# Cross-attention with fake quantisation on one core: TensorE's work grouped by array shape, one accumulator bank, three score banks

## What is computed

```python
q = _fq_sym(q, axis=-1); k = _fq_sym(k, axis=-1); v = _fq_sym(v, axis=2)
attn = jnp.einsum('bhqd,bhkd->bhqk', q, k)
attn = jax.nn.softmax(attn.astype(jnp.float32), axis=-1)
attn = _fq_unsigned(attn, axis=-1)        # round(attn / (rowmax / 255)), clipped to 0..255
out = jnp.einsum('bhqk,bhkd->bhqd', attn, v)
```

## Time and profile before

| | |
|---|---|
| median of 3 runs | 9790.67 us (9786.69 to 9797.47) |
| profiled execution | 9785.63 us, span 9783.8 us |
| TensorE busy by the profile | 9016.5 us, 92% |
| VectorE busy | 6668.5 us, 68% |
| ScalarE busy | 6056.4 us, 62% |
| GpSimd busy | 5207.5 us, 53% |
| DMA | 303.96 MB, mean 31 GB/s |

### The profile page before, as it was taken

How to read it: one execution, slowest core, us unless ns; L and a number is a source line. 1 busy time by engine, 2 the same in 40 slices (tenths; PEclk the granted TensorE clock), 3 DMA queues, 4 the chain that set the end, 5 groups by cost and what they waited for, 6 DMA issues and landing times.

```text
span 9783.8 us, 225157 instructions
## 1 busy us (share of the span) xinstructions
PE 9016.5 (92%) x60844; PEld 2698.2 (28%) x60844; DVE 6668.5 (68%) x6162; ACT 6056.4 (62%) x12203; POOL 5207.5 (53%) x3575
## 2 busy tenths in 40 slices
PE   8935999999999999999999999999999999998688
PEld 4501222222222222222222222222222222222243
DVE  8968777767776777677767776777767776730266
ACT  2300767767676767676767676776767676767333
POOL 5723555555555555555555555555555555555266
PEclk9955999999999999999999999999999999999799
DMA  5662010110101010101010101010110101010100
GB/s 167 198 137 67 10 24 18 22 18 16 25 15 26 10 31 10 31 10 31 10 30 11 30 11 25 16 23 18 19 22 17 25 10 30 11 28 6 26 4 3
DMA packets 305415, 303.96 MB, mean 31 GB/s; under 512 B 50718, under 2 KB 297802, under 8 KB 300458
## 3 DMA queue, kind: packets, MB, share of 16 engines
q1 hardware_dynamic: 304682, 303.13, 14.2%
q10 hardware_dynamic: 672, 0.16, 0.0%
HBM read 226.31 MB, written 76.71 MB: 31 GB/s over the span
## 4 chain that ended last, share of the span: by engine, by line
PE 84%; issue 6%; DVE 5%; ACT 2%; POOL 2%; DMA 1%; SPq 0%; DVEq 0%; ACTq 0%; POOLq 0%
PE psum L1385 32%; PE psum L1354 23%; PE psum L1308 15%; PE psum L1364 8%; DVE mpart L1171 3%; PE psum L1273 2%; ACT y L1068 1%; POOL mix L410 1%; PE psum L670 1%; PE psum L1406 1%; DVE act_c L550 1%; PE psum L1342 1%; PE psum L1344 0%; PE psum L643 0%; PE psum L1285 0%
## 5 line engine op out<-in xcount | busy, mean ns | idle before, releaser
L1171 DVE TENSOR_REDUCE mpart<-psum 128x978 f32 x4992 | 5768.0, 1175 | 2194.0 <-PE psum L1308 2193.3
L1068 ACT ACTIVATE y<-psum 128x400 f32<-128x400 f32 x11520 | 5638.0, 503 | 2338.9 <-PE psum L1385 1875.5
L986 POOL TENSOR_SCALAR xh<-y 128x1600 f16<-128x1600 f32 x2880 | 4397.8, 1527 | 3666.0 <-ACT y L1068 3666.0
L1385 PE MATMUL psum<-QT,K 99*128 x11520 | 3811.3, 344 | 142.3 <-ACT y L1068 62.6
L1354 PE MATMUL psum<-y,ones 128*1 128x400 f32 x23056 | 2517.3, 503 | 0.6 <-ACT y L1068 0.6
L1308 PE MATMUL psum<-K,QS 48*128 48x489 bf16 x9984 | 1974.8, 392 | 266.1 <-DVE mpart L1171 194.8
L1385 PEld LDWEIGHTS psum<-QT,K 99*128 x11520 | 1041.3, 96 | 3722.2 <-issue 3629.4
L1364 PE MATMUL psum<-xh,vwin 128*16 128x400 f16 x11532 | 1000.7, 338 | 0.0
L1308 PEld LDWEIGHTS psum<-K,QS 48*128 48x128 bf16 x9984 | 482.3, 93 | 1366.4 <-issue 791.5
L1354 PEld LDWEIGHTS psum<-y,ones 128*1 128x1 f32 x23056 | 322.0, 81 | 577.8 <-issue 571.4
L1364 PEld LDWEIGHTS psum<-xh,vwin 128*16 128x16 f16 x11532 | 274.7, 85 | 557.2 <-issue 546.1
(11 more groups left out here) (184 smaller groups left out, 2380.1 us busy)
## 6 DMA issues: line engine op xcount, KB each, us to landing
K<-kT_parts SPq DMA_DIRECT2D x204, 240.0 KB, 8.3
vwin<-v_int SPq DMA_DIRECT2D x579, 80.0 KB, 1.9
K<-kT_parts SPq DMA_DIRECT2D x772, 45.8 KB
kT_parts<-part SPq DMA_DIRECT2D x135, 256.0 KB, 3.2
K<-kT_parts SPq DMA_DIRECT2D x102, 242.0 KB, 8.5
src<-in_ctx_dram SPq DMA_DIRECT2D x46, 512.0 KB, 4.5
v_float<-kv SPq DMA_DIRECT2D x45, 512.0 KB, 5.2
vin<-v_float SPq DMA_DIRECT2D x9, 2560.0 KB, 13.1
```

Of the source, the lines that this page charges most:

```text
L986: pool.tensor_scalar(xh[:, g % YR, :, :], y[:, g % YR, :, :], INT_STEP, 0.0, ALU.mult, ALU.add)\
L1068: act.activation(y[:, s % YR, j, :], s2_bank(j), ACT.Exp).then_inc(exp_done, 1)
L1171: dve.tensor_reduce(mpart[:, t, ds(2 * cp + j, 1)], s1_buf(n)[:, :, 0:CHALF], AX.XY, ALU.max)\
L1385: pe.matmul(s2_bank(j), K3[0:MROW, h % 2, ds(c * REGION + t * P, P)], queries, start=True, stop=True).then_inc(s2_ready, 1)
```

## The change

- TensorE's order in a group becomes: two scores, the group's one or two jobs, two scores, sums, values.
- The ring of score banks grows from two to three (`S2_RING`, banks 4 to 6), so that a score waits for the exponential of three tiles before.
- ScalarE takes the exponentials of three tiles with two instructions: one over two banks (800 elements per partition), one over a single bank.
- Sums and values share one accumulator bank (`ACC`, bank 7). The ones become a matrix of 17 columns, 16 of them zero, so that the sum comes out on row 16 of each strip, beside the values' rows 0 to 15, and adds zero to these.
- One copy (`acc_s`) in place of two at a block's start, and one product in place of two for each sequence in `turn_out`.
- Rings of three groups in place of five, lags of 1 and 2 groups in place of 2 and 3.
- The constants at the start are set accordingly.

```diff
-YR = 5
-LAG_SUM, LAG_PV = 2, 3
+YR = 3
+LAG_SUM, LAG_PV = 1, 2
+S2_RING = 3
...
+        def s2_banks(t, count):
+            return psum[:, 4 + t % S2_RING:4 + t % S2_RING + count, 0:QB]
+
         def s2_bank(j):
-            return psum[:, 4 + j % 2, 0:QB]
-
-        PV, SUM = psum[:, 6, 0:QB], psum[:, 7, 0:QB]
+            return psum[:, 4 + j % S2_RING, 0:QB]
+
+        ACC = psum[:, 7, 0:QB]
...
-                for s in range(GROUPS):
-                    if not later and s == LAG_SUM:
+                def group_start(s):
+                    if not later and s == LAG_PV:
 
                         act.wait_ge(summed, YR + groups_before(h, b, 0))
+                        act.wait_ge(pv_done, YR + groups_before(h, b, 0))
                         act.wait_ge(rsum_done, block_of(h, b))
-                        act.activation(sum_s[:], SUM, ACT.Copy).then_inc(evicted, 1)
-                    if not later and s == LAG_PV:
-                        act.wait_ge(pv_done, YR + groups_before(h, b, 0))
-                        act.activation(pv_s[:], PV, ACT.Copy).then_inc(evicted, 1)
+                        act.activation(acc_s[:], ACC, ACT.Copy).then_inc(evicted, 1)
 
                     act.wait_ge(summed, groups_before(h, b, c) + s + 1)
                     act.wait_ge(rounded_y, groups_before(h, b, c) + s + 1)
-                    for j in range(GT):
-                        act.wait_ge(s2_ready, tiles_before(h, b, c) + GT * s + j + 1)
-                        act.activation(y[:, s % YR, j, :], s2_bank(j), ACT.Exp).then_inc(exp_done, 1)
+
+                rows = y[:].rearrange("p r t q -> p (r t) q")
+                for t in range(0, BTILES, S2_RING):
+                    for first, count in ((t, 2), (t + 2, 1)):
+                        for u in range(first, first + count):
+                            if u % GT == 0:
+                                group_start(u // GT)
+                        act.wait_ge(s2_ready, tiles_before(h, b, c) + first + count)
+                        at = first % (YR * GT)
+                        act.activation(rows[:, at:at + count, :], s2_banks(first, count), ACT.Exp).then_inc(exp_done, count)
...
-                    pe.matmul(s1_buf(n)[0:SEQ, 0, 32 * s:32 * s + HD], pv_s[:, s * SEQ:(s + 1) * SEQ], sel[:, 0:HD],
-                              start=True, stop=True, skip_group_check=True)
-                    last = pe.matmul(s1_buf(n)[0:SEQ, 0, 32 * s + HD:32 * s + HD + 1], sum_s[:, s * SEQ:(s + 1) * SEQ],
-                                     sel[:, HD:HD + 1], start=True, stop=True, skip_group_check=True)
+                    last = pe.matmul(s1_buf(n)[0:SEQ, 0, 32 * s:32 * s + HD + 1], acc_s[:, s * SEQ:(s + 1) * SEQ], sel[:],
+                                     start=True, stop=True, skip_group_check=True)
...
-                    last = pe.matmul(SUM[32 * j:32 * j + 1, :], ones[:], y[:, g % YR, j, :],
+                    last = pe.matmul(ACC[32 * j:32 * j + HD + 1, :], ones[:], y[:, g % YR, j, :],
                                      start=(start and j > 0), stop=True, skip_group_check=True)
...
-                    last = pe.matmul(PV[32 * j:32 * j + HD, :], vwin[:, g % GROUPS // 5, GT * (g % 5) + j, :],
+                    last = pe.matmul(ACC[32 * j:32 * j + HD, :], vwin[:, g % GROUPS // 5, GT * (g % 5) + j, :],
                                      xh[:, g % YR, j, :],
-                                     start=(start and j > 0), stop=True, skip_group_check=True)
+                                     start=False, stop=True, skip_group_check=True)
...
                     score_tile(s, 0)
+                    score_tile(s, 1)
+                    next_jobs(JOBS_AT[s])
+                    score_tile(s, 2)
+                    score_tile(s, 3)
+
                     g = s - LAG_SUM
                     if not later and g == 1:
-
-                        pe.wait_ge(evicted, 2 * block_of(h, b) + 1)
-                        pe.wait_ge(exp_done, 2 + T)
-                        pe.matmul(SUM[0:1, :], ones_x[:], yx[:], start=True, stop=True, skip_group_check=True)\
+                        pe.wait_ge(evicted, block_of(h, b) + 1)
+                        pe.wait_ge(exp_done, S2_RING + T)
+                        pe.matmul(ACC[0:HD + 1, :], ones_x[:], yx[:], start=True, stop=True, skip_group_check=True)\
                             .then_inc(summed_x, 1)
                         sum_group(T, 0, True)
                     if later or g != 0:
                         sum_group(T, g, False)
-                    score_tile(s, 1)
-                    if s not in SINGLE:
-                        next_jobs(1)
-                    score_tile(s, 2)
-                    if s in SINGLE:
-                        next_jobs(1)
                     g = s - LAG_PV
...
                     if later or g != 0:
-                        value_group(body_of(h, b, c), g, False)
-                    score_tile(s, 3)
-                    next_jobs(JOBS_AT[s] - 1)
+                        value_group(body_of(h, b, c), g)
```

## The result

The changed kernel takes 9884.69 us (median of 4, 9872.78 to 9907.04) against 9788.68 us before (median of 4): ratio 1.0099, 95% interval 1.008 to 1.0118. It is slower by 1%, where I had forecast 9466, which is 3.3% faster.

What follows compares the result with a forecast made beforehand. TensorE was taken as the bound, losing time to shape changes. Sixty blocks with jobs at -5.6 us (-334), the last head +19 and head ends -10 gave -325: 9466 us on the median, 8-in-10 range 9300 to 9650.

Steps and rivals of the forecast that it cites:

- U to V: On TensorE, a group's sums (U) followed by its values (V): taken as free of shape-change cost, V 0.66 us after U.
- rival A: Going from sums to values on TensorE costs a whole shape change, 0.12 us in 2880 groups: 9811 us; chance 5%.
- rival B: The pair exponential on ScalarE costs two singles, 1.01 us: +0.16 in nearly all groups, 9926 us; chance 5%.
- the new wait: TensorE's scores wait for the pair exponential to free its banks: 0.4 us in ten groups of fifteen.
- rival C: The new waits lower TensorE's granted clock beyond head starts: 9650 us; 10%, together with part of rival A, beyond 9570.
- VectorE's delay: A job waits for VectorE's reduction, late by up to 0.35 us, hidden inside tile 3's 0.4 wait; costed at nothing.
- the third kind: Every third group (2, 5 and so on), waiting only for a single exponential: 2.35 us with two jobs, 2.235 with one.
- 39.3 + 2.7: Within a block with jobs: one body of 15 groups at 39.3 us plus the block's own steps at 2.7.
- The terms for the last head: The head without jobs: groups from 2.47 to 2.575 us plus 0.02, +4.7 per block, +19 us for four.
- the head's end: TensorE's 3.6 us wait for the maxima at a head's end: 0.7 of it used, 15 times, -10 us.
- the rule's 2.745: Forecast length in us of groups of the first two kinds, where scores wait for the pair exponential.
- an ideal of 34.4: Body time in us if only shape changes counted and no score waited: gain 6.4 per body, 8560 us overall; 2%.

## Why the prediction was wrong

**What held.** TensorE bound the kernel before; a change of shape costs 0.11 and scores side by side stand 0.17 apart; four changes fewer per group; U to V is no change of shape, so rival A is out (V starts 0.69 after U. U with 17 columns takes 0.80 to a score across a change of shape in the run of single exponentials in the old order, which less 0.11 is the same 0.69); the pair lasts 0.84 (rival B as worded is out); the new wait stands at tile 3 and at tile 6, in two groups of three; the clock stays (rival C is out: 0.99 in the heads with jobs before and after, 0.97 and 0.96 in the last head, and the slices of the earlier trace rows are unchanged; a fall of the clock did come in the written-out bodies, behind a stop of 2.9 us, not behind the waits of 0.4); VectorE's delay lies inside the wait.

**What failed** is one step, the length of that wait, in the sentence "0.38 + 0.84 + 0.14 = 1.36 after the start of its second score" and in the 0.17 behind it. The wait is where I put it, but the chain through it is longer, 0.44 + 0.84 + 0.19 and then 0.27. Four terms of the group were too small:

| term | forecast | measured, second and third body |
|---|---|---|
| score to exponential | 0.38 | 0.44 for the pair, 0.38 for a single |
| end of exponential to score | 0.14 | 0.19 to 0.20 (0.14 in the first body) |
| the waiting score to the next | 0.17 | 0.27 |
| U to V, V to S | 0.66, 0.28 | 0.69, 0.28 |

Together 0.24 in ten groups of fifteen. They have three causes:

- The register operation gives 0.15 of it, 0.05 in the release and 0.10 between the two scores. The 0.17 came from two scores behind a sum, where the queue had time to run ahead. The 0.14 did come from behind a real wait, but in a body of the last head, where the operation lasts 46 ns. In two of three bodies of the heads with jobs it lasts 103, and the difference is the 0.05 that is missing.
- The late start of the pair, 0.06, is there with constant addresses too (4307.21 against a second score at 4306.77), so it is not register work. Its cause is open.
- The sums, 0.03: I took 0.13 for a change of shape out of the 0.79 of the earlier trace rows, where my own price of a change was 0.11.

With the third kind at 2.50 and 2.32 for 2.35 and 2.235, a second body takes 42.08, not the 39.3 that I took between 38.97 and 39.7. Two such bodies are 5.6 us longer than forecast. The rest of the block, a first body of 42.6 and the extra tile's score, takes 43.3 where the sum had 39.3 + 2.7. That is the 7 us by which the block is longer than forecast, and 60 blocks make nearly all of the 419 us between 9466 and 9885. The terms for the last head (its first three blocks are 26 us longer by the starts of their first products, where I had 19 for four) and for the head's end (0.1 us shorter, where I had 0.7) were off too, by some 10 us each.

That the register work costs this is shown by the pair of runs with zeros: 11344 register operations and 9887 us, none for these scores and 9411. It is shown for the 0.15, not for the 0.06 and the 0.03. Without the operations the rule's 2.745 holds by errors that cancel: the pair's start is still 0.44 after the second score and the sums are 0.69, which is 0.09 more, and the release is 0.05, which is 0.09 less. I had seen the sign of it in the rows of before. The one-job group took 2.53 where the rule gave 2.48, and I put half of the 0.06 into the sum without asking what it was. The trace of before answers it. A one-job group in a first body, with 46 ns, and one in a second body, with 103, from sums to sums:

```profile
2138.49 0.85 PE L1354 MATMUL psum<-y,ones 128*1 128x400 f32 x8
...
2140.97 0.85 PE L1354 MATMUL psum<-y,ones 128*1 128x400 f32 x8
```

```profile
2179.22 0.85 PE L1354 MATMUL psum<-y,ones 128*1 128x400 f32 x8
...
2181.75 0.85 PE L1354 MATMUL psum<-y,ones 128*1 128x400 f32 x8
```

2.48 and 2.53: the difference is that of the two operations. (The group of the earlier trace rows itself lies at the turn from a first to a second body, where its last step is longer.) The change puts such a wait into most groups.

**Which rival it became.** None of mine. The time of the new wait was on record as a loss of 5 us per body from an ideal of 34.4, which should have been a rival with a point from which it decides: 325/2880 = 0.11 us per group more and nothing is gained. I had worked out this very number for rival B, and had tied it to one cause, the pair's duration, instead of to every term of the chain from the second score to the fourth.

**And the ideal.** "That the waits vanish" had 2% and 8560 us; without the pair the kernel stands at 8870 with rings of five and at 8895 with rings of three. That is some three quarters of the 1225 us of the ideal, when single exponentials free the banks one by one.

## What to carry to other kernels

When an engine that ran ahead begins to wait, price the wait by its whole chain: start behind the producer, work, release, the queue's own register work, and the distance to the next instruction; take each from a place where the engine really waits, and in a loop whose addresses come from the same registers, since the same wait in another loop nest had a shorter operation behind it. An instruction over two buffers saves ScalarE time that this kernel did not lack, and frees both at its end; look at what waits for the first of them before you merge. A control that is to bring back a cost must be checked in its trace to have brought it back.

## What the runs showed of the hardware that I had not expected

- TensorE's queue spends 46 or 103 ns on a register operation in front of a score whose operand address a register gives. Behind a wait the score starts 0.05 us after the exponential's end with a constant address, 0.14 with the first, 0.19 to 0.20 with the second. The constant addresses were tried with zeros, but the kernel before has the case with its real data as well: in the first bodies of the last head, without the operation, the score starts 0.06 after the exponential's end. Where the queue runs ahead, neither shows (two-job groups of before, 2.79 us with the operations and without).
- Addresses that recur in a body cost no further operation: four different addresses per body left 816 such operations where 60 left 11344.
- A two-bank exponential of 800 elements starts 0.44 us after the second score, a single 0.38, and the pair split into two singles starts after 0.38 too. Why was not tried.
- Writing two loop bodies out raised instruction transfers from 0.33 to 11.5 MB on one queue, put a stop of 2.9 us and some groups at the lower clock at each block's start, and the total stayed where it was, 9880 for 9885 us. That the stop is an instruction fetch was not tried.
